# Four layers on eight images: a new order of TensorE's work around a selective scan, with the scan's row load in two parts

## The reference

```python
xz = silu(einsum('oc,bchw->bohw', in_proj_w, x) + in_proj_b)      # 1536 x 512
x_ssm, res, gate = split(xz, 3, axis=1)
xf = silu(depthwise_conv3(x_ssm) + dw_b)                          # along the 1024 positions
x_h = take_along_axis(xf.reshape(B, 2, 256, N), perm)             # two heads, each its own order
dbc = (einsum('oc,bcn->bon', dbc_w, xf) + dbc_b)                  # per head: dt, B (8), C (8)
dt = softplus(dbc[:, :, 0]);  B_t, C_t = dbc[:, :, 1:9], dbc[:, :, 9:17]
dt, B_t, C_t = (gather by perm)
# scan over positions: h = exp(dt*A) * h + dt*B * x ;  y = C . h + D * x
y = gather(y_h, inverse perm).reshape(B, 512, H, W)
y = y * silu(gate) + res
out = silu(einsum('oc,bchw->bohw', out_proj_w, y) + out_proj_b)
```

## Time and profile before

| | us |
|---|---|
| Median of three runs | 1747.64 |
| The profiled execution's own time | 1750.19 |
| Its span | 1748.4 |
| TensorE busy | 1651.4 (94%) |
| VectorE busy | 1147.0 (66%) |
| ScalarE busy | 892.9 (51%) |
| GpSimd busy | 413.1 (24%) |
| Mean granted TensorE clock | 0.984 |

### The profile page before, as it was taken

The page is one execution under the profiler, slowest core; times in us unless marked ns, Lnnn a source line. Parts: engine busy times, 40 slices in busy tenths (PEclk is TensorE's granted clock), DMA queues, the critical chain, the costliest instruction groups (busy, mean ns, idle before and its releaser), DMA issues.

```text
span 1748.4 us, 24401 instructions
## 1 busy us (share of the span) xinstructions
PE 1651.4 (94%) x8693; PEld 927.0 (53%) x8693; DVE 1147.0 (66%) x2472; ACT 892.9 (51%) x1091; POOL 413.1 (24%) x423
## 2 busy tenths in 40 slices
PE   4689899999999999999999999999999999999988
PEld 3254554555545655456545565455554565545643
DVE  6878776557855676647865568565775576662775
ACT  4647353565355654455634645356525555445542
POOL 0304311044021331133220341204402142113220
PEclk9889999999999999999999999999999999999999
DMA  6203410134102331223211341023410233112301
GB/s 207 94 0 103 145 28 13 73 127 145 40 25 89 114 118 40 74 92 105 95 21 73 127 139 34 14 85 120 140 40 36 84 117 109 40 48 75 102 25 49
DMA packets 124078, 140.16 MB, mean 80 GB/s; under 512 B 52259, under 2 KB 101475, under 8 KB 123950
## 3 DMA queue, kind: packets, MB, share of 16 engines
q1 hardware_dynamic: 109902, 103.18, 18.6%
q0 software_dynamic: 12288, 34.68, 5.9%
q10 hardware_dynamic: 1760, 0.64, 0.2%
HBM read 78.46 MB, written 60.01 MB: 79 GB/s over the span
## 4 chain that ended last, share of the span: by engine, by line
PE 64%; DVE 10%; issue 9%; POOL 9%; DMA 4%; ACT 3%; SPq 0%; DVEq 0%; POOLq 0%; ACTq 0%
PE bank L1618 61%; POOL d_scan L463 6%; DMA rows<-d_y,rank 1%; POOL rows L480 1%; DVE bn L913 1%; DMA d_y<-buf_b 1%; PE bank L1786 1%; POOL work L469 1%; DVE gate L1136 1%; PE bank L1917 1%; PE bank L1837 1%; DVE res L1260 1%; DVE res L1258 1%; DMA rows<-d_scan 1%; ACT res L643 1%
## 5 line engine op out<-in xcount | busy, mean ns | idle before, releaser
L1618 PE MATMUL bank<-buf_a,win_hi 128*128 128x512 f16 x1536 | 461.9, 383 | 8.2 <-DVE buf_a L985 8.1
L1618 PE MATMUL bank<-buf_a,win_lo 128*128 128x512 f16 x768 | 293.6, 382 | 0.0
L1618 PE MATMUL bank<-buf_b,w_hi 128*128 128x512 f16 x960 | 288.1, 382 | 2.3 <-DVE buf_b L985 2.3
L1618 PEld LDWEIGHTS bank<-buf_a,win_hi 128*128 128x128 f16 x1536 | 149.5, 99 | 174.5 <-DVE buf_a L985 10.9
L463 POOL DMA_INDIRECT d_scan<-rows,rank x128 | 125.3, 979 | 347.3 <-ACT rows L648 304.7
L1618 PE MATMUL bank<-buf_b,w_lo 128*128 128x512 f16 x480 | 183.2, 382 | 0.0
L1618 PE MATMUL bank<-buf_a,w_hi 128*128 128x512 f16 x576 | 171.3, 379 | 1.4 <-DVE x_odd L1228 1.3
L1618 PEld LDWEIGHTS bank<-buf_b,w_hi 128*128 128x128 f16 x960 | 94.0, 99 | 112.5 <-DVE buf_b L985 3.0
L480 POOL DMA_INDIRECT rows<-d_y,rank x128 | 125.8, 983 | 97.8 <-DMA d_y<-buf_b 61.6
L1618 PEld LDWEIGHTS bank<-buf_a,win_lo 128*128 128x128 f16 x768 | 75.7, 99 | 92.4 <-issue 3.0
L1618 PE MATMUL bank<-gate,w_out 128*128 128x512 f32 x256 | 120.2, 602 | 1.1 <-DVE gate L1341 1.1
(11 more groups left out here) (253 smaller groups left out, 3068.9 us busy)
## 6 DMA issues: line engine op xcount, KB each, us to landing
rows<-d_scan SPq DMA_DIRECT2D x16, 1092.0 KB, 5.8
d_y<-buf_b SPq DMA_DIRECT2D x64, 256.0 KB, 2.2
work<-in_x SPq DMA_DIRECT2D x24, 512.0 KB, 4.5
d_gram<-rows SPq DMA_DIRECT2D x32, 260.0 KB, 2.4
x_even<-in_x SPq DMA_DIRECT2D x16, 512.0 KB, 5.5
x_odd<-in_x SPq DMA_DIRECT2D x16, 512.0 KB, 5.4
out_x<-x_even SPq DMA_DIRECT2D x16, 512.0 KB, 3.1
out_x<-x_odd SPq DMA_DIRECT2D x16, 512.0 KB, 2.6
```

Of the source, the lines that this page charges most:

```text
L1618: return eng.matmul(out, lhsT, rhs, start=start, stop=stop, skip_group_check=True, **kw)
```

## The change

Six things are moved or split; no arithmetic changes.

1. TensorE issues five quarter units instead of four ahead of the last `tokens(3)`, and 19 + 12 instead of 20 + 16 between it and the first `scan_sums(0)`: the first sums stand one unit sooner. Between the inner part of head 1 and its outputs stand two quarter units instead of six. Twelve instead of four stand behind the first four `y_chunk`s.
2. The transpose for the bound moves into the outputs of head 1 (`bound_across`), the matmul for it behind the first `y_chunk`.
3. `in_bank` and `out_bank`: units 17 to 23 alternate between banks 2 and 1.
4. SyncE loads a head's rows in two DMAs, the last 17 columns first (`scanrows`), then the 256 of x (`scanx`), for which the first state product waits.
5. ScalarE: one unit fewer is evacuated before the scan, the copies of head 0's outputs stand one place sooner among the exponentials of head 1, and the last evacuations alternate with `y_high`.
6. VectorE: `scan_blocks(0)` ahead of `scan_masks(1)`, and `scan_states(1)` ahead of `y_largest`.

```diff
-        in_bank = (3, 4, 6, 1, 2, 1, 2, 1, 2, 1, 4, 5, 6, 3, 2, 1, 4, 5) + (2, 1) * 3
-        out_bank = (0, 1, 2, 5, 6, 0, 3, 4)
+        in_bank = (3, 4, 6, 1, 2, 1, 2, 1, 2, 1, 4, 5, 6, 3, 2, 1, 4) + (2, 1) * 3 + (2,)
+        out_bank = (0, 2, 1, 5, 6, 0, 3, 4)
@@ SyncE
-                    eng.dma_start(rows4[:, h], d_scan[h].rearrange("(c p) r -> p c r", p=P)).then_inc(s[f"scanrows{h}"], 16)
+                    stored = d_scan[h].rearrange("(c p) r -> p c r", p=P)
+                    eng.dma_start(rows4[:, h, :, DH:ROW], stored[:, :, DH:ROW]).then_inc(s[f"scanrows{h}"], 16)
+                    eng.dma_start(rows4[:, h, :, 0:DH], stored[:, :, 0:DH]).then_inc(s[f"scanx{h}"], 16)
@@ ScalarE
-                    filler(4)
+                    filler(3)
                 else:
-                    filler(9)
+                    filler(8)
@@
+                scan_y(0, 0)
                 scan_exp(1, 0)
+                scan_y(0, 1)
                 scan_exp(1, 1)
-                scan_y(0, 0)
+                scan_y(0, 2)
                 scan_exp(1, 2)
-                scan_y(0, 1)
                 scan_decays(1)
-                scan_y(0, 2)
                 scan_y(0, 3)
                 scan_factors(1)
-                filler(3)
+                filler(2)
                 for j in range(4):
                     scan_y(1, j)
                 y_high(m, 0)
                 y_high(m, 1)
                 filler(1)
                 y_high(m, 2)
+                filler(1)
                 y_high(m, 3)
+                filler(1)
@@ VectorE
+                scan_blocks(m, 0)
                 scan_masks(m, 1)
-                scan_blocks(m, 0)
...
                 scan_blocks(m, 1)
+                scan_states(m, 1)
                 y_largest(m)
-                scan_states(m, 1)
@@ TensorE
                 tokens(2)
-                filler(1)
+                piece(KC + 1)
                 tokens(3)
-                filler(5)
+                piece(5 * KC - 1)
                 if not (first or last):
                     gn_sum(m + 1, 0)
-                filler(4)
+                filler(3)
@@ in factor_rows
-                        wait(eng, "in_evac", m, 18)
+                        wait(eng, "in_evac", m, 17)
@@ in state_products
+                        if c == 0:
+                            wait(eng, f"scanx{h}", m, 16)
@@
+                def bound_across():
+
+                    wait(eng, "w_maxc", m, ROUNDS + 1)
+                    eng.transpose(bound_row, y_bound[:, 7:8], ident).then_inc(s["w_maxt"], 1)
+
-                def scan_y(h):
+                def scan_y(h, between=None):
 
                     r = rows4[:, h]
                     for c in range(NT):
+                        if c == NT - 2 and between:
+                            between()
@@
                 scan_inner(1)
-                wait(eng, "w_maxc", m, ROUNDS + 1)
-                eng.transpose(bound_row, y_bound[:, 7:8], ident).then_inc(s["w_maxt"], 1)
-                piece(6)
-                wait(eng, "w_maxr", m, 2 * ROUNDS + 3)
-                mm(bound_all, const("ones")[0:1, :], y_bound[0:1, 1:2], True, True).then_inc(s["w_maxb"], 1)
-                scan_y(1)
+                piece(2)
+                scan_y(1, bound_across)
@@
                 for n in range(4):
                     y_chunk(*gate_order[n])
-                piece(4)
+                    if n == 0:
+                        wait(eng, "w_maxr", m, 2 * ROUNDS + 3)
+                        mm(bound_all, const("ones")[0:1, :], y_bound[0:1, 1:2], True, True).then_inc(s["w_maxb"], 1)
+                piece(12)
```

More of the change, by code:

```diff
@@ L207, in build @@
             l0_done l0_evac l0_add_pool l0_add_dve in_done in_evac out_done out_evac out_add l2_done l2_add l3_done l3_add
-            conv_pad conv_mac conv_act tok_mm tok_ev dbc_mm sp_z sp_dve sp_act row_ready scattered0 scattered1 scanrows0 scanrows1
+            conv_pad conv_mac conv_act tok_mm tok_ev dbc_mm sp_z sp_dve sp_act row_ready scattered0 scattered1 scanrows0 scanrows1 scanx0 scanx1
             fac_mv fac_c fac_mm fac_arg fac_exp fac_gam fac_pq fac_8 fac_diag fac_tp fac_ptq mm_m m_ev dh_mm h_zero h_st y_mm y_ev y_out0 y_out1 y_in00 y_in01 y_in10 y_in11
@@ L218, in build @@
                    conv_pad=1, conv_mac=3 * KC, conv_act=KC, tok_mm=KC, tok_ev=KC, dbc_mm=1, sp_z=1,
-                   sp_dve=10, sp_act=2, row_ready=1, scattered0=16 * NT, scattered1=16 * NT, scanrows0=16, scanrows1=16,
+                   sp_dve=10, sp_act=2, row_ready=1, scattered0=16 * NT, scattered1=16 * NT, scanrows0=16, scanrows1=16, scanx0=16, scanx1=16,
                    fac_mv=3 * HEADS, fac_c=(T8 + 1) * HEADS, fac_mm=HEADS, fac_arg=3 * HEADS, fac_exp=3 * HEADS, fac_gam=HEADS, fac_pq=3 * HEADS,
```

## The result

| | before | after |
|---|---|---|
| Median of four runs each, us | 1747.29 | 1775.2 (1770.3 to 1777.15) |
| The profiled execution's own time, us | 1750.19 | 1775.99 |
| Mean granted TensorE clock | 0.984 | 0.976 |

The ratio of after to before is 1.0137, 95% interval 1.0083 to 1.0191. It is a ratio of means: one of the four runs before took 1761.05 us, the other three 1746.6 to 1747.64, so the medians lie 1.6% apart. The forecast was 1750 us with a range up to 1766; the time lies 25 us above the one and 9 above the other.

A forecast was written before the change was run, and what follows sets the result against it. TensorE, at work nearly all the time, was taken as the bound, movable only by idle stretches and clock. Idle changes of -2 us and clock of +5 gave +3 on the median 1747.64: 1750 us, range 1736 to 1766.

The forecast's parts named there:

- Steps One: TensorE up to the first scan sums: a fifth quarter unit fills the 0.34 us hole; sums start at 784.4.
- Three: ScalarE, head 1's exponentials: earlier copy removes a 1.72 us wait, exposes the 1.28 us table load; chain gains 1.6 us.
- Five: TensorE from head 0's outputs: new 0.6 us wait in head 1's outputs, 2.5 us idle before the third gather-transpose block.
- Step Two: Split row load: small part takes 3 us, masks are done before TensorE asks at 784.4; cost nothing.
- Step Four: Head 0's gather: eighth starts at 822.2, is used 2.90 us after its start, complete at 825.1 to 825.2.
- rival of the late gather: Next image's loads, issued as the eighth gather starts, make landing 4.4 us instead of 2.9; 1767 us; chance 0.12.
- Step Seven: TensorE's clock falls behind the new wait in five or six of eight images: 8 us against 3 now, +5.

The follow-up runs named there:

- e10: The kernel before with only the row load split in two parts, small part first: 1730.64 us, ratio 0.9882.
- e1: The changed kernel with the next image's four loads held until both halves of head 0's gather have landed: 1763.69 us, ratio 1.006.
- e3: The changed kernel with 16 useless matmuls of 512 columns ahead of the third block of gather transposes: 1763.74 us, ratio 1.0057.
- e9: The kernel before with only ScalarE's copies of head 0's outputs one place sooner among head 1's exponentials: 1756.17 us, ratio 1.0021.
- e4: The changed kernel with ScalarE's first exponential of head 1 ahead of the first output copy again: 1741.88 us, ratio 0.9945.
- e8: The changed kernel with exponentials ahead of copies and four quarter units moved ahead of the gather wait, loads unchanged: 1719.29 us, ratio 0.9819.

## Why the prediction was wrong

**Where the wait comes: right.** Steps One, Three and Five hold to a few tenths. The copy starts 1.49 us after the first outputs (1.6 forecast), the load takes 1.28, the first exponential starts at 811.33 - 8.13 = 803.2 as forecast, the diagonal and the eighth gather too. The load starts 0.02 us after the copy ends (810.02 and 810.04), and the activation begins 0.01 us after the load: from the copy's end to the activation 1.31 us, where the step had 1.3. There is no wait at the second gather, and the sums start one unit sooner.

**Step Two, the split: right for head 0** (2.4 us for the small rows, forecast 3; masks at 790.60 - 8.13 = 782.5 as forecast) and wrong in what it is worth. I costed it as a cover for head 0's masks and noted only in passing that VectorE no longer waits for head 1's. e10 shows that this second effect, alone, fills the whole 12.2 us of holes that the new order of the copies was to fill: the best part of the change stood in the sum at nothing. This did not move the forecast, which counted the same holes as filled by the order of the copies; it hid that the new order was not needed for them. Given the split, everything else in the change costs 1775.2 - 1730.6 = 45 us.

**Step Four, the landing: the step that failed.** It took 2.90 us from a gather that was issued at 836.26, when the next image's loads, issued from 829.65, were nearly through. The eighth gather of the new order has the loads right behind it and takes 5.86. The rival of the late gather named this mechanism and priced it at 4.4 us and 12 + 9 us in all (for eight images, though the last has no loads), with a chance of 0.12; the argument against it was the same row. Measured: from issue to use 4.6 to 6.2 us in the seven images with loads, mean wait 4.3 instead of 2.5, 34.6 - 20 = 14.6 us. e1 gives 8.6 us of wait back by moving only the loads, so they are shown for over half of it. The rest of the surplus is open: in the last image, without such loads, it is still 3.62 us against 2.90.

**Step Seven, the clock: mechanism right, size off.** Forecast were five or six falls of 1.5 us; it was eight, and one costs 2.9 us in the fourth image (11.6 less 8.7) at a wait of 5 us. In three of the eight windows the fall is shorter. e3 measures 17 to 20 us for all, where the step had 8. The price came from two windows of 3.6 us with clocks of 0.60 and 0.54, behind waits of some 2 us; TensorE did 10 and 13 instructions in them, against 16 at 1.00 behind a wait of 1.98. The 1.5 us was the author's estimate, six or seven matmuls of 0.22 us, and no run shows it as such; the fourth image shows 2.9 in its place, with the clock at 0.50 for the whole window and on to about 842.

**The sum again**, with these two terms: from the forecast without any clock loss (1742.6), + 14.6 for the landing and + 17 to 20 for the clock: 1774 to 1777; measured 1775.2. That it closes so well is in part luck. The growth in the profiled executions is 13.8 us of idle and 11.9 of busy time, where the forecast had -2 and +5: the idle part is the forecast with the landing to about 1 us, the busy part some 7 us over the forecast, where 17 to 20 instead of 8 would be 9 to 12. The new wait of 0.6 us in each image was in the forecast.

The chance of slower by over 1%, 0.09, was far too low. Once a wait stands with nothing behind it to fill it, its length, its clock cost and its eight repetitions all err to the same side.

## What to carry to other kernels

Take the landing time of a transfer from a row with the same neighbours in the queues, not from the same instruction in a quieter stretch (5.86 us and 2.90 here), and count a wait of some microseconds on TensorE at about one and a half times its length where matmuls follow, as here (5.05 us of wait and 2.9 of clock). Before reordering around a hole, ask what the late engine itself waits for: splitting off the 6% of a load that its first consumer reads gained 21 us with a few lines, where the new order of the copies only moved the hole (e9). A copy that isn't ready must not stand ahead of a change of function tables; put the load where the engine is idle anyway. Here the load of 1.28 us stood behind 5.05 us of idle time in after and within the idle time in e4, where the first exponential came 1.6 us sooner.

## What the runs showed of the hardware

- From issue to use a gather of 128 rows took 2.90 us where the next image's loads were nearly through the earlier trace rows, 3.62 with output writes and no such loads (last image of after), 3.6 to 5.0 with the loads held (e1), and 4.6 to 6.2 with four loads of 512 KB issued 0.6 to 0.7 us behind it (after). With these loads held, the gather of the fourth image was used 3.92 us after its issue instead of 5.90 (e1): loads that were issued after it had delayed it. The gap alone doesn't set it: one image of e8 took 5.86 with the loads 1.55 us behind. Nor did the loads gain: in the fourth image their median to landing was 6.6 us against 4.9 in the kernel before.
- 1,024 runs of 68 bytes landed in 2.4 us, while 1,024 runs of 1,024 bytes took 6.2 (medians of 16, after).
- With the DMA engines at a share of 1.01, TensorE did 21 instructions in 3.6 us at a clock of 1.00 (e3), and with a share of 1.02 it did 13 at 0.50 (after): what looked like contention in the second was the clock.
- Behind waits of 2 to 2.7 us the clock did both. It fell behind 1.97 us (before, at 1013.8), 2.24 and 2.62 (e3) and 2.44 (e4), and stayed up behind 1.98 (before, at 395.1), 2.31 (e3) and 2.69 (e4). Behind 5.05 us it fell and cost 2.9.
